# A transformer block on one core: five weight loads moved behind the first row reads, a modulation in ten pieces, scores head by head in two batches, and weight splits on GpSimd

## The chip, the cores and the metric

The kernel runs on one core of one Trainium2 chip. The metric is the time of one execution in device microseconds; lower is better. The core has five engines that run their own instruction lists and meet at semaphores: TensorE (PE; its weight loads are listed as PEld), VectorE (DVE), ScalarE (ACT), GpSimd (POOL) and SyncE (SP), which here only issues transfers.

## What is computed

One block of a conditioned transformer over 32 batches of 256 rows and 288 channels, in float32 precision (16 heads of 18 columns, inner width 1152):

```
ada = silu(c) @ W_ada + b_ada                 # c: one row of 288 for each batch
shift_msa, scale_msa, gate_msa, shift_mlp, scale_mlp, gate_mlp = split(ada, 6)
h = layernorm(x) * (1 + scale_msa) + shift_msa
q, k, v = split(h @ W_qkv + b_qkv)
attn = softmax(q * 18**-0.5 @ k.T)            # for each of 16 heads, 256 x 256
x = x + gate_msa * ((attn @ v) @ W_proj + b_proj)
h = layernorm(x) * (1 + scale_mlp) + shift_mlp
x = x + gate_mlp * (gelu(h @ W_fc1 + b_fc1) @ W_fc2 + b_fc2)
```

## The kernel before, in words

Float32 products are made of rounded parts: every operand is a rounded high part (`hi`) and the remainder (`lo`), and a product is high by high, high by low and low by high. So each weight is loaded in 12 transfers or groups of transfers (`loads`, numbered 0 to 11: 0 to 2 for W_qkv, 3 to 5 for W_proj, 6 to 8 for W_fc1, 9 to 11 for W_fc2), rounded on ACT (`round`) and split on DVE (`split`, L1035, or L1033 for the remainder rows 2, 5 and 8). All twelve loads are issued by SP before anything else of the batches; the loads 3 to 11 stand between the second batch's x and the first write of q and k.

A batch goes through steps that every engine knows by name. `ln1_stats` and `ln1_apply` normalise x; `xt` turns it on PE (L742, L745) and applies the modulation on ACT (L909); DVE and POOL make high and low parts (`xt` on these, POOL L1262). `qk` makes q and k (PE L768, 14 matmuls for a pair of tiles, ACT L918, DVE L1120), `v` makes v (L776). q and k are then written to memory as rows (`qkw`, SP L597, five writes) and read back in another layout (`qkr`, 24 reads, L613; six of those of the first half of batch 0 are issued by ACT, L990), `ql` and `kl` being the tiles that they land in. `s` is one pair of heads: four matmuls into two banks, head i of the pair in row half i of the array (L793). `max` is a head's maximum on DVE (L1128), `mt` turns the maxima and `mb` copies them into `ql` on ACT (L935), after which `st` (L810) makes the transposed scores, ACT the exponentials (L942) and `pv` (L822) the sums with v. `proj`, `lt`, `fc1`, `fc2` are the rest of the block.

`mod` is the second modulation (the columns of shift_mlp and scale_mlp for all batches) and `gate2`, `gate5` are the gates, all of them products of silu(c) with W_ada on PE (L715, L729). The first modulation is made by the same function before the batches begin. The first `st` waits for `gates_ready` and for both modulations.

The order in which each engine takes its steps is written out by hand in tables: a head for the first three periods (`PE_HEAD`, `ACT_HEAD`, `DVE_HEAD`, `POOL_HEAD`, `SYNC_HEAD`), a period that is repeated for the batches in the middle, and a tail. An engine never takes a step out of this order.

## Time and profile before

| | us |
|---|---|
| median of 3 runs | 1203.75 (1203.28 to 1208.13) |
| the profiled execution | 1203.89 |
| its span in the profile | 1202.1 |
| PE busy in the span | 1158.4 (96%) |
| DVE busy | 920.6 (77%) |
| ACT busy | 858.0 (71%) |
| POOL busy | 579.2 (48%) |
| mean granted TensorE clock | 0.984 of full speed |

The span is what the profile records of one execution. The time around it is 1.8 us. A share of busy time is a mean over stages which have different limits, so each stage is to be read by itself. The granted clock is a fraction of TensorE's upper level: 1.00 is the level of 2.4 GHz and 0.50 that of 1.2 GHz.

### The profile page before, as it was taken

Reading aid. Unit: us, or ns where it says so; the run is one execution under the profiler, and the core shown is the slowest. Engines: PE = TensorE matmul, PEld = TensorE weight load, DVE = VectorE, ACT = ScalarE, POOL = GpSimd, SP = SyncE. Lnnn points to the kernel's source line nnn. Section 1 sums busy time; section 2 is a strip of 40 time slices with the busy share of each in tenths; the row PEclk is TensorE's granted clock in tenths of the full one; section 3 lists DMA queues with packets and bytes.
Section 4 is the critical chain, followed back from the end, with each engine's and each line's share of the span. In section 5 each row is a group of like instructions: output and inputs, shape, how many; then the busy total and the mean of one; then the engine's idle time right before and its main releaser. Section 6 shows DMA issues by size and latency. Waiting matters only on the chain.

```text
span 1202.1 us, 28774 instructions
## 1 busy us (share of the span) xinstructions
PE 1158.4 (96%) x10375; PEld 993.9 (83%) x10375; DVE 920.6 (77%) x1928; ACT 858.0 (71%) x1485; POOL 579.2 (48%) x619
## 2 busy tenths in 40 slices
PE   6888999999999999999999999999999999999987
PEld 5666788888888888888888888888888888888777
DVE  5578878878878788887778888877888887877553
ACT  4378777777777777777777787777777777778721
POOL 3012444555544445554454555445455544544664
PEclk9779999999999999999999999999999999999999
DMA  9454554455555445555544555555445555444220
GB/s 276 137 172 156 163 164 147 150 175 168 164 159 163 149 148 173 166 171 164 163 151 151 159 179 165 165 159 167 143 149 181 164 165 161 158 148 156 83 68 20
DMA packets 133814, 186.93 MB, mean 156 GB/s; under 512 B 24284, under 2 KB 102150, under 8 KB 133675
## 3 DMA queue, kind: packets, MB, share of 16 engines
q1 hardware_dynamic: 133513, 184.66, 48.9%
q8 instruction: 84, 1.38, 0.5%
q10 hardware_dynamic: 162, 0.44, 0.1%
q14 instruction: 55, 0.45, 0.1%
HBM read 119.92 MB, written 64.60 MB: 153 GB/s over the span
## 4 chain that ended last, share of the span: by engine, by line
PE 92%; DVE 3%; ACT 2%; DMA 1%; issue 1%; SPq 0%; POOL 0%; ACTq 0%; POOLq 0%; DVEq 0%
PE a_bank L855 13%; PE x_bank L768 12%; PE turn_bank L822 10%; PE b_bank L855 9%; PE score_bank L793 7%; PE st_bank L810 7%; PE b_bank L869 7%; PE b_bank L870 6%; PE b_bank L871 6%; PE a_bank L836 5%; PE x_bank L776 5%; PE x_bank L742 2%; PE a_bank L742 1%; ACT e L942 1%; PE x_bank L745 1%
## 5 line engine op out<-in xcount | busy, mean ns | idle before, releaser
L1128 DVE TENSOR_REDUCE mx<-score_bank 128x2 f32<-128x512 f32 x512 | 332.3, 685 | 94.6 <-PE score_bank L793 92.8
L942 ACT ACTIVATE e<-st_bank 128x1024 f32<-128x1024 f32 x256 | 262.3, 1024 | 163.9 <-PE st_bank L810 163.3
L1285 POOL TENSOR_TENSOR gl<-gl_raw,gh 128x512 fp32r<-128x512 f32 (+1 forms) x160 | 197.2, 1241 | 180.8 <-DVE gh L1193 180.8
L935 ACT CAST ql<-mxt 4x256 fp32r<-4x256 f32 x512 | 205.7, 402 | 5.3
L869 PE MATMUL b_bank<-w,gh 128*128 128x288 f32 x576 | 179.1, 311 | 2.0 <-DVE tmp L1199 1.9
L870 PE MATMUL b_bank<-w,gh 128*128 128x288 f32 x576 | 170.6, 296 | 0.0
L871 PE MATMUL b_bank<-w,gl 128*128 128x288 f32 x576 | 169.6, 295 | 0.0
L822 PE MATMUL turn_bank<-e,ve 128*32 128x256 f32 x2048 | 125.8, 387 | 0.1
L810 PE MATMUL st_bank<-ql,kl 58*128 58x256 f32 x1024 | 117.9, 309 | 6.1 <-ACT e L942 5.0
L793 PE MATMUL score_bank<-kl,ql 58*128 58x256 f32 x1024 | 120.7, 314 | 2.7 <-DVE mx L1128 1.9
L855 PE MATMUL a_bank<-xh,w 128*128 128x256 f32 x640 | 112.2, 298 | 5.5 <-DVE xr L1107 4.0
L869 PEld LDWEIGHTS b_bank<-w,gh 128*128 128x128 f32 x576 | 108.6, 189 | 8.1 <-DVE tmp L1199 2.6
L1297 POOL TENSOR_TENSOR x<-tmp,x 128x288 f32<-128x288 f32 x64 | 52.0, 813 | 129.7 <-DVE tmp L1199 129.5
L768 PE MATMUL x_bank<-xh,wq 128*128 128x256 f32 x632 | 111.9, 300 | 2.2 <-DVE qst L1120 1.3
L1193 DVE CAST gh<-gl_raw 128x512 fp32r<-128x512 f32 (+1 forms) x160 | 92.7, 594 | 23.0 <-ACT gl_raw L980 22.0
L870 PEld LDWEIGHTS b_bank<-w,gh 128*128 128x128 f32 x576 | 108.7, 189 | 0.0
L871 PEld LDWEIGHTS b_bank<-w,gl 128*128 128x128 f32 x576 | 108.6, 189 | 0.0
L855 PEld LDWEIGHTS a_bank<-xh,w 128*128 128x128 f32 x640 | 87.4, 191 | 25.4 <-issue 15.1
L768 PEld LDWEIGHTS x_bank<-xh,wq 128*128 128x128 f32 x632 | 87.6, 193 | 20.2 <-issue 16.0
L793 PEld LDWEIGHTS score_bank<-kl,ql 58*128 58x128 f32 x1024 | 78.4, 188 | 30.9 <-issue 19.9
L810 PEld LDWEIGHTS st_bank<-ql,kl 58*128 58x128 f32 x1024 | 78.0, 187 | 29.8 <-issue 15.5
L822 PEld LDWEIGHTS turn_bank<-e,ve 128*32 128x32 f32 x2048 | 60.5, 111 | 43.9 <-issue 6.7
(152 smaller groups left out, 2490.9 us busy)
## 6 DMA issues: line engine op xcount, KB each, us to landing
qk_rows<-qst SPq DMA_DIRECT2D x128, 256.0 KB, 3.7
ql<-qk_rows SPq DMA_DIRECT2D x384, 72.0 KB
kl<-qk_rows SPq DMA_DIRECT2D x378, 72.0 KB
o_rows<-on SPq DMA_DIRECT2D x128, 128.0 KB
gate<-gates SPq DMA_DIRECT2D x32, 432.0 KB, 4.5
xin<-in_x SPq DMA_DIRECT2D x32, 288.0 KB, 4.1
x<-in_x SPq DMA_DIRECT2D x32, 288.0 KB, 4.0
out<-x SPq DMA_DIRECT2D x32, 288.0 KB, 2.2
```

The lines of the kernel that those rows point to most:

```text
L768: last = nc.tensor.matmul(bank[:, k * L:(k + 1) * L], wa[:, c * P:(c + 1) * P], xa, start=(i == 0), stop=(i == len(pr) - 1))
L793: last = nc.tensor.matmul(score_bank[i][:, t * L:(t + 1) * L], ql[rows, slot, j % HP, t * P:(t + 1) * P], kl[rows, slot, j % HP, :], start ...
L810: last = nc.tensor.matmul(st_bank[:, i, u, :], kl[rows, slot, j % HP, u * P:(u + 1) * P], ql[rows, slot, j % HP, :], start=True, stop=True)
L822: last = nc.tensor.matmul(turn_bank[VB * c:VB * (c + 1), q * L:(q + 1) * L], ve[:, b % 2, u, 8 * half + 2 * c + q, :], e[:, c, q, u, :], s ...
L855: last = nc.tensor.matmul(bank[:, (f % 2) * L:(f % 2 + 1) * L], wa[:, f * P:(f + 1) * P], xa, start=(i == 0), stop=(i == len(pr) - 1))
L869: nc.tensor.matmul(b_bank[:, 0:C], gh[:, cols], w2[:, 0, f, :], start=(f == 0), stop=False)
L870: nc.tensor.matmul(b_bank[:, 0:C], gh[:, cols], w2[:, 1, f, :], start=False, stop=False)
L871: last = nc.tensor.matmul(b_bank[:, 0:C], gl[:, cols], w2[:, 0, f, :], start=False, stop=(f == NF - 1))
L935: last = nc.scalar.copy(rows[:, :, :, a, :], src)
L942: nc.scalar.activation(e[:, j % 4, :, :, :].rearrange("p i u l -> p (i u l)"), st_bank[:, :, :, :].rearrange("p i u l -> p (i u l)"), ACT. ...
L1128: nc.vector.tensor_reduce(mx[:, j // HP, i, :, col:col + 1], score_bank[i][:, :].rearrange("p (t l) -> p t l", t=NT), AX.X, ALU.max).then_ ...
L1285: nc.gpsimd.tensor_tensor(gl[:, cols], g[:, cols], gh[:, cols].bitcast(F32), ALU.subtract).then_inc(g_lo, 1)
```

## The change

The tables of the head are rewritten, the periods and the tail are not. SP issues the loads 3 to 6 ahead of the batches and the loads 7 to 11 at places in its table. The second modulation is made in ten pieces, each of which is a step. The scores of the batches 0 and 1 are made by `sh`, one head at a time. Of the splits that stood in DVE's table only those of the remainder rows (5 and 8) stay there; the seven others are POOL's. In the function that makes a modulation, the three copies of the last 32 columns (`r`), which were the innermost loop, are now outside the loop over the rows of W_ada (`k`); the first modulation runs through it too.

```diff
-        N_FIRST = 3
+        N_FIRST, N_EARLY = 3, 7
...
-            for i in range(N_FIRST, len(loads)):
+            for i in range(N_FIRST, N_EARLY):
                 load_weights(i)
...
-            def mod_columns(n):
-                for i in range(2):
-                    c0 = MOD_OF[2 * n + i] * C
-                    for c in range(3):
-                        for k, (_r, nr) in enumerate(K_ROWS):
-                            rows = nr + (k == 2)
-                            for r in range(1 if c < 2 else 3):
-                                to = mod_of[n][:, i, c, :] if c < 2 else mod_of[n][REM * r:REM * (r + 1), i, c, :]
-                                cols = slice(c0 + c * P, min(c0 + (c + 1) * P, c0 + C))
-                                last = nc.tensor.matmul(to, w_ada_sb[k][0:rows, cols], sT[0:rows, k, :],
-                                                        start=(k == 0), stop=(k == 2))
-                last.then_inc(ada_mod, 1)
+            def mod_piece(n, i, c, r):
+                c0 = MOD_OF[2 * n + i] * C
+                cols = slice(c0 + c * P, min(c0 + (c + 1) * P, c0 + C))
+                for k, (_r, nr) in enumerate(K_ROWS):
+                    rows = nr + (k == 2)
+                    to = mod_of[n][:, i, c, :] if c < 2 else mod_of[n][REM * r:REM * (r + 1), i, c, :]
+                    last = nc.tensor.matmul(to, w_ada_sb[k][0:rows, cols], sT[0:rows, k, :],
+                                            start=(k == 0), stop=(k == 2))
+                return last
+            MOD_PIECES = [(i, c, r) for i in range(2) for c in range(3) for r in range(1 if c < 2 else 3)]
+            def mod_columns(n):
+                for i, c, r in MOD_PIECES:
+                    last = mod_piece(n, i, c, r)
+                last.then_inc(ada_mod, 1)
...
+            def s_head(b, h):
+                j, i = h // 2, h % 2
...
+                wait(pe, s_max[i], PAIRS * b + j)
+                rows = slice(TILE * i, TILE * i + KM)
+                for t in range(NT):
+                    last = nc.tensor.matmul(score_bank[i][:, t * L:(t + 1) * L],
+                                            ql[rows, slot, j % HP, t * P:(t + 1) * P], kl[rows, slot, j % HP, :],
+                                            start=True, stop=True)
+                last.then_inc(s_full[i], 1)
...
             def fc1(b, n):
                 if b == 0 and n == 0:
-                    act.wait_ge(w_split, len(loads))
+                    act.wait_ge(w_split, 5)
+                    act.wait_ge(w_late, 7)
...
+            def split_late(_b, i):
+                _kind, _w, _bias, raw, hi, lo, _n, _k = loads[i]
+                pool.wait_ge(w_hi, i + 1)
+                nc.gpsimd.tensor_tensor(lo, raw, hi.bitcast(F32), ALU.subtract).then_inc(w_late, 1)
```

The tables are shown by the instructions that they give, without those that come again. On PE, in the stretch that ends with the first scores, the kernel before has these rows (L715 is the second modulation, L745 the second part of `xt` of batch 1, L793 the first pair of scores):

```order
L715 MATMUL st_bank<-rcb,e 128x32 x2
L715 MATMUL st_bank<-rcb,gh_raw_56 128x32
L715 MATMUL st_bank<-rcb,e 128x32 x2
L715 MATMUL st_bank<-rcb,gh_raw_56 128x32
L715 MATMUL st_bank<-rcb,e 32x32 x6
L715 MATMUL st_bank<-rcb,gh_raw_56 32x32 x3
L745 MATMUL x_bank<-ident,xn 96x128 x2
L729 MATMUL a_bank<-e,rcb 32x288
L793 MATMUL score_bank0<-kl,ql 128x256
L793 MATMUL score_bank1<-kl,ql 128x256
L793 MATMUL score_bank0<-kl,ql 128x256
L793 MATMUL score_bank1<-kl,ql 128x256
```

The changed kernel has there (L718 is the modulation, L756 and L759 are `xt`, L743 the gates, L782 is `qk` of batch 1, L825 the new step for one head):

```order
L756 MATMUL x_bank<-ident,xn 128x128 x4
L718 MATMUL st_bank<-rcb,e 128x32 x2
L718 MATMUL st_bank<-rcb,gh_raw_56 128x32
L718 MATMUL st_bank<-rcb,e 32x32 x2
L718 MATMUL st_bank<-rcb,gh_raw_56 32x32
L759 MATMUL x_bank<-ident,xn 96x128 x2
L743 MATMUL a_bank<-e,rcb 32x288
L743 MATMUL b_bank<-e,rcb 32x288
L782 MATMUL x_bank<-xh1,wq 128x256 x4
```
```order
L782 MATMUL x_bank<-xl1,wq 128x256 x2
L782 MATMUL x_bank<-xr1,wq 128x256
L825 MATMUL score_bank0<-kl,ql 128x256 x2
L825 MATMUL score_bank1<-kl,ql 128x256 x2
L825 MATMUL score_bank0<-kl,ql 128x256 x2
```

Ahead of these one wide piece of the modulation now stands before `v` of batch 0. Two pieces are left between the two parts of `xt`, where ten were, and the other seven come after the first scores. The first scores stand behind the first 14 matmuls of `qk` of batch 1, where they stood ahead of them.

On SP, around the writes of q and k of batch 0, the kernel before has (L554 to L568 are loads of weights, L597 are the writes, L613 the reads, L573 are x of the batches 2 and 3):

```order
L554 DMA w1_raw_51<-in_L0_cond_W_fc1 128x1152 x2
L563 DMA gl_raw_57<-in_L0_cond_W_fc1 32x1152 x3
L565 DMA gl_raw_57<-in_L0_cond_b_fc1 1x1152 x2
L568 DMA w2_raw_52<-in_L0_cond_W_fc2 128x3x288 x3
L573 DMA xin<-in_x 128x576
L597 DMA qk_rows<-qst 128x2x256 x4
L597 DMA qk_rows<-qst 64x2x256
L613 DMA ql<-qk_rows 18x1024 x6
```

and the changed kernel (L560, L569 and L571 are the loads 7 and 8, L603 are writes, L619 reads, L579 is x):

```order
L603 DMA qk_rows<-qst 128x2x256 x2
L579 DMA xin<-in_x 128x576
L603 DMA qk_rows<-qst 128x2x256
L619 DMA ql<-qk_rows 18x1024
L579 DMA xin<-in_x 128x576
L603 DMA qk_rows<-qst 128x2x256
L619 DMA ql<-qk_rows 18x1024
L603 DMA qk_rows<-qst 64x2x256
L619 DMA ql<-qk_rows 18x1024 x4
L560 DMA w1_raw_51<-in_L0_cond_W_fc1 128x1152
L569 DMA gl_raw_57<-in_L0_cond_W_fc1 32x1152 x3
L571 DMA gl_raw_57<-in_L0_cond_b_fc1 1x1152 x2
```

Load 6 stands right ahead of these rows. So ten rows of weight transfers are gone from the place ahead of the writes. One of the loads of 128 by 1152 and the five small ones stand behind the first six reads, the loads of W_fc2 further on.

On POOL, at the layer norm and the turning of the batches 2 and 3, the kernel before has (L1236 are the inverse deviations that `ln1_apply` waits for, L1262 is `xt`, L1232 clears `ql`):

```order
L1262 TENSOR_TENSOR xl1<-xl1_raw_53,xh1 128x512
L1240 COPY mod1<-mod 128x6
L1236 TENSOR_TENSOR rs1<-ve1,mhalf 128x2
L1240 COPY mod1<-mod 128x6
L1236 TENSOR_TENSOR rs1<-ve1,mhalf 128x2
L1262 TENSOR_TENSOR xl1<-xl1_raw_53,xh1 128x512
L1232 MEMSET ql 68x1024 x2
L1262 TENSOR_TENSOR xl1<-xl1_raw_53,xh1 128x512
```

and the changed kernel (L1270 are the inverse deviations, L1301 is `xt`, L1297 the new split):

```order
L1297 TENSOR_TENSOR wp<-wp_raw_50,wp 126x288 x2
L1301 TENSOR_TENSOR xl1<-xl1_raw_53,xh1 128x512
L1274 COPY mod1<-mod 128x6
L1270 TENSOR_TENSOR rs1<-ve1,mhalf 128x2
L1301 TENSOR_TENSOR xl1<-xl1_raw_53,xh1 128x512
L1297 TENSOR_TENSOR w1<-w1_raw_51,w1 128x1152
L1274 COPY mod1<-mod 128x6
L1270 TENSOR_TENSOR rs1<-ve1,mhalf 128x2
L1297 TENSOR_TENSOR w1<-w1_raw_51,w1 128x1152
L1266 MEMSET ql 68x1024 x2
L1301 TENSOR_TENSOR xl1<-xl1_raw_53,xh1 128x512
```

So POOL has four splits of weights more in this stretch, two of them 1152 wide; the three splits of W_fc2 come later, the last one right behind the inverse deviations of batch 0's second layer norm.

## Rows read from the trace of the kernel before

**Rows 1.** Stretches of the span: length, each engine's busy time (instructions), granted clock, DMA share, GB/s.
```profile
20.00:30.00 10.00, 7.41 (x47) 6.26 (x45) 4.61 (x14) 2.25 (x5) 0.69 (x1) 1.00 1.05 283
30.00:45.00 15.00, 11.56 (x76) 9.32 (x77) 1.99 (x5) 2.41 (x5) 1.57 (x2) 0.56 0.56 151
45.00:58.00 13.00, 10.59 (x64) 7.43 (x62) 11.95 (x30) 6.58 (x13) 0.69 (x1) 0.89 0.38 118
58.00:73.00 15.00, 14.42 (x86) 9.35 (x86) 10.89 (x21) 10.28 (x19) 2.96 (x4) 0.51 0.57 177
93.00:140.00 47.00, 40.31 (x381) 30.69 (x380) 40.52 (x81) 38.97 (x71) 13.78 (x16) 0.96 0.48 151
140.00:1150.00 1010.00, 1007.43 (x9227) 872.36 (x9226) 801.76 (x1672) 762.41 (x1319) 521.37 (x547) 1.00 0.50 158
```

**Rows 2.** Chain that ended last, 6 to 24 us: start, length, what.
```profile
14.56 0.23 DVE xn L1056
...
14.84 1.13 PE x_bank L742 x4
...
17.22 0.65 PE x_bank L745 x2
...
18.66 3.24 PE x_bank L768 x14
```

**Rows 3.** The same chain over the whole span, two of its longest pieces.
```profile
25.17 6.93 DMA qk_rows<-qst
34.53 7.16 PE st_bank L715 x60
```

**Rows 4.** Instructions in time, 33 to 59 us: start, length, engine, line, what [idle before].
```profile
33.44 1.09 PE L742 MATMUL x_bank<-ident,xn 128*128 128x128 f32 x4 [4.67 <-ACT ve L924]
...
41.62 0.66 PE L745 MATMUL x_bank<-ident,xn 128*96 128x128 f32 x2
...
43.31 0.80 PE L793 MATMUL score_bank<-kl,ql 58*128 58x256 f32 x4
...
45.91 0.82 DVE L1041 BATCH_NORM_STATS2 stat<-xin 128x6 f32<-128x288 f32 x2
...
54.62 0.31 DVE L1137 STREAM_TRANSPOSE mxt<-mx 128x128 f32<-128x128 f32 x1
...
58.32 0.80 PE L810 MATMUL st_bank<-ql,kl 58*128 58x256 f32 x4
```

**Rows 5.** PE in time in the first modulation, two groups of narrow matmuls.
```profile
10.23 0.43 PE L715 MATMUL turn_bank<-rcb,e 128*32 128x32 f32 x12
10.60 0.33 PE L715 MATMUL turn_bank<-rcb,gh_raw 33*32 33x32 f32 x6
```

**Rows 6.** DVE by line and shape, 20 to 140 us: busy, mean ns, idle before.
```profile
L1128 DVE TENSOR_REDUCE mx<-score_bank 128x2 f32<-128x512 f32 x58 | 37.9, 684 | 11.7 <-PE score_bank L793 11.1
...
L1035 DVE TENSOR_TENSOR w<-w_raw,w 128x864 fp32r<-128x864 f32 x3 | 3.2, 1050 | 0.0
...
L1035 DVE TENSOR_TENSOR w<-w_raw,w 128x1152 fp32r<-128x1152 f32 x2 | 2.7, 1346 | 0.0
```

**Rows 7.** DVE and POOL in time, 67 to 70 us.
```profile
67.49 1.27 POOL L1262 TENSOR_TENSOR xl<-xl_raw,xh 128x512 fp32r<-128x512 f32 x1
67.63 2.18 DVE L1054 TENSOR_SCALAR xn<-xin,mv,rs 128x288 f32<-128x288 f32 x1 [0.21 <-POOL rs L1236]
...
68.70 0.94 POOL L1232 MEMSET ql<- 68x1024 f32 x1
```

**Rows 8.** A late row read on SP and the PE instruction that waited for it.
```profile
114.68 0.47 SPq L613 DMA_DIRECT2D kl<-qk_rows  x1
...
118.49 0.50 PE L793 MATMUL score_bank<-kl,ql 58*128 58x256 f32 x4 [0.65 <-DMA kl<-qk_rows]
```

**Rows 9.** DMA issues: size each, median us from issue to landing.
```profile
qk_rows<-qst SPq DMA_DIRECT2D x128, 256.0 KB, 3.7
```

**Rows 10.** L793 alone in 20 ns at the start of a pair of heads.
```profile
74.00:74.02 0.02, 0.01 (x2) 0.01 (x2) 1.00 0.00 0
```

125 lines of the change are left out of this document (70 added, 55 removed), and 56 rows, old and new, of tables (ACT_HEAD, DVE_HEAD, PE_HEAD, POOL_HEAD).

## The prediction

> **What bounds the kernel now.** I read the profile in this order: busy time by stretch, the chain that ended last, then instructions in time where the two show waits.
>
> In the stretch from 140 to 1150 us TensorE is busy 1007.4 of 1010 us at full clock [rows 1]. The tables of the periods and of the tail are the same in both kernels, so whatever TensorE reaches that stretch early or late by, the end moves by. The change can act only on the first 140 us. There the reader is to see three things. From 30 to 45 us the granted clock is 0.56, DVE works 2.0 and ACT 2.4 us of 15: all stand behind something. From 45 to 58 us DVE is busy 11.95 of 13 us and carries the stretch. From 58 to 73 us TensorE is busy 14.4 of 15 us, but at a granted clock of 0.51, the level of 1.2 GHz. From 93 to 140 us TensorE leaves 6.7 of 47 us idle and DVE 6.5 [rows 1].
>
> What all stand behind between 25 and 43 us is in the chain: the third write of q and k starts at 25.17 and takes 6.93 us, to 32.1; further on the second modulation takes 7.16 us in one piece [rows 3]. The DMA share between 20 and 30 us is 1.05, so the queues are full of weights [rows 1]. The median write of this kind lands in 3.7 us [rows 9]. In time: `xt` of batch 1 starts on TensorE at 33.44 after an idle time of 4.67 us, its second part at 41.62, the first scores at 43.31, DVE's first transposed maxima at 54.62, the first `st` at 58.32 [rows 4].
>
> **The change part by part.** Sums are made against the profiled execution, 1203.89 us, which is 0.1 us over the median shown.
>
> *The first modulation, a cost that the words of the change don't name.* The loop order changed: the three copies of the last 32 columns now follow one another, where they alternated. Alternating, 18 narrow matmuls of one half go in 0.7 us, 0.04 us each [rows 5]; the second modulation has 60 matmuls in 7.16 us, 36 of them narrow, so the 24 wide ones take (7.16 - 1.4) / 24 = 0.24 us each [rows 3, 5]. Narrow ones in a row that don't overlap cost between 0.04 (nothing changes) and 0.24 us (as a wide one). A narrow load has a quarter of the columns, so I take 0.06: 36 x 0.06 - 1.4 = 0.8 us. Nothing hides it: TensorE takes up `xt` at 14.84, right behind DVE's 14.56 + 0.23 [rows 2]. Term +0.8, bounds 0 and 7.
>
> The Trainium skill, "TensorEngine Tiling (Array Packing)", section Key Properties, says that different tiles of the array load weights and multiply in parallel. Rows 10 agree: two matmuls of a pair of heads and both their weight loads are in flight in the same 20 ns. By that rule alone both the narrow copies and the heads taken singly lose their overlap.
>
> *Five loads behind the reads.* By their shapes they take some 2.4 MB off the queues ahead of the writes. With an empty queue the third write takes the median 3.7 us instead of 6.93 [rows 3, 9]: with the 0.8 us above it lands at 25.17 + 0.8 + 3.7 = 29.7 instead of 32.1. The median is one of queues that are half busy (DMA share 0.50 in the steady stretch [rows 1]), so a little less is possible; the other bound is 6.93 (the queue isn't what held it).
>
> *The modulation in pieces.* `xt` of batch 1 started 1.3 us after the landing [rows 3, 4], so now at 31.0. Between its parts stood 8.2 us, 7.16 of them modulation [rows 3, 4]; one wide and one narrow piece are left, 1.0 us at this clock, and ACT has to take up the first part behind its 1.09 us on TensorE. So its second part comes at about 33.2. ACT still has to issue the last row read of the first half behind this, at about 34.5. A read issued at 114.68 freed its waiter at 118.49, 3.8 us later [rows 8]. So the reads have landed at 38.3. TensorE meanwhile does `qk` of batch 1: at the beginning 1.44 us lay between the second part of `xt` and `qk`, which took 3.24 us [rows 2]; 33.2 + 4.7 = 37.9, hidden behind the reads. First score 38.3 instead of 43.31: **-5.0 us**. Bounds: -7 (the reads have landed sooner and `qk` runs at the upper level in half of its 3.24 us) and 0.
>
> *From the first score to the first `st`*, 15.0 us [rows 4]. DVE carries it. The statistics of batch 2 (0.82 us and two small ones) and a split of 1.35 us [rows 4, 6] go out of it, some 2.5 us. Against it the gates on DVE now stand behind two wide and several narrow pieces on TensorE, which has 2.4 us idle in the stretch [rows 1]. **-2.0**, bounds -3 and +1.
>
> *Splits off DVE after that.* One of 1.35 and three of 1.05 us: 4.5 us [rows 6]. DVE is idle for 14% of 93 to 140 us [rows 1], and its in-order queue is only one of the three that TensorE waits for: I take 0.4 of it, **-1.7**, bounds -4.5 and 0.
>
> *The same splits on POOL.* 512 columns take 1.27 us there [rows 7], so 1152 take 2.9, 864 take 2.1 and 288 take 0.7: 13.5 us for seven. POOL is 48% busy and its queue is short here; the first GELU, which waits for all seven, is the last but one of ACT's steps in the head. But DVE is held: an operation from SBUF to SBUF, begun at 67.63, took 2.18 us and ended at 69.81, as POOL's two operations ended at 69.64 [rows 7]. The new splits of 2.9 and 2.1 us stand behind the inverse deviations that `ln1_apply` of batch 3 and `ln2_apply` of batch 0 wait for, so these meet them. Maxima read PSUM and aren't held: their mean over 58 groups is 685 ns with POOL busy or not [rows 6]. I take four meetings of 1 us, half of it on the path: **+2.0**, bounds 0 and 8.
>
> The Trainium skill, "SBUF — State Buffer", section "SBUF: two separate sides", says that the port pair that both engines share is an exclusive lock for a whole instruction, against a DVE operation in a two-port mode or with two SBUF inputs. By that rule the price of a meeting is up to the whole of POOL's 2.9 us; the trace agrees with the 2.18 us row.
>
> *Scores head by head.* A head waits for its own bank, not for both. DVE waited 11.1 us for scores between 20 and 140 us [rows 6]. Against it, TensorE pays for the lost overlap of a pair: two matmuls run at once before [rows 10]. **-1.5**, bounds -5 and +2.
>
> The steady stretch takes all of it over: -5.0 - 2.0 - 1.7 + 2.0 - 1.5 = -8.2 (the 0.8 is in the first term). 1203.9 - 8.2 = **1195.7**; I say 1195.5.
>
> **The rivals.**
>
> *More comes than the sum has: the clock stays up.* TensorE waits less between 25 and 45 us. If the stretch that ran at 0.51 with 14.4 us of work [rows 1] runs at the upper level, 7 us of work vanish, of which I count 4: 1191.5, down to 1185. Against it: in the stretch at 0.51 TensorE was 96% busy, so waits alone don't decide the level. Chance 0.17.
>
> *Given back on the way to 140 us.* POOL's lock at its full price: three meetings of 2.9, 2.9 and 2.1 us on the path, 7.9 instead of 2.0, gives 1195.5 + 5.9 = 1201.4. For it: the split of 2.9 us follows at once on the deviations. Or the stretch from 93 us on is set by ACT, whose work is unchanged (39.0 of 47 us busy, as much as DVE [rows 1]), and only the first term's half survives: about 1200. Chance 0.25.
>
> *The change doesn't do what it says:* the third write takes its 6.9 us also with the loads gone, because the first loads are still in the queues. Then the landing is at 32.9 and the first score 3 us later than I say: 1198.5. Held with the one above in the 0.25.
>
> *Slower: the clock falls for longer.* The work between 45 and 58 us ran at 0.89 (10.6 us busy) and that from 93 to 140 us at 0.96 (40.3 us busy) [rows 1]. Each us of it that runs at the lower level costs one more. To be slower than before by over 0.5% it has to cost 14 us above the sum, so more than 14 us of that work has to fall: with the first stretch at 0.5 and a tenth of the second, 1210 to 1214. For it: scores in single heads leave small gaps on TensorE. Against it: from 93 us on it was at 0.96 although TensorE idled 14% of the time. Chance 0.08.
>
> **How the numbers follow.** The sum's own case has 0.50 and runs from 1191.5 to 1199. Likeliest 1195.5. The range takes in the half of the better case and most of the given-back one: 1187 to 1201.5. A measurement of this kernel tells about 0.5% (6 us) from no change, so faster is below 1197.7: most of the main case (0.47) and the better one (0.17), 0.64; within 0.5% 0.28; slower 0.08.
>
> **What would show it.** Right: the third write lands near 30 us; `xt`'s second part at 33, first score near 38, first `st` near 51; the first modulation ends 0.8 us later; TensorE is saturated 8 us earlier and the steady period is unchanged. Wrong, if: `sh` waits for row reads behind the loads 7 and 8; DVE operations of over 2 us stand beside POOL's splits and a TensorE wait follows them; the granted clock shows more than some 30 us at 0.5 before 140 us; or the first modulation grew by several us.

## The result, and the profile after

The changed kernel takes 1220.76 us (median of 6 runs, 1215.02 to 1221.74) against 1203.93 us of the kernel before on the same chip: a ratio of 1.0123, 95% interval 1.0098 to 1.0148. It is 15 us slower. The forecast said 8 us faster, with a range of 1187 to 1201.5. The profiled execution took 1220.11 us, with a span of 1218.3.

The stretches of the kernel after, with the columns of [rows 1]:

```profile
20.00:30.00 10.00, 9.07 (x52) 8.33 (x52) 5.52 (x16) 2.83 (x6) 2.63 (x4) 1.00 0.35 110
30.00:45.00 15.00, 9.19 (x56) 6.57 (x56) 4.95 (x13) 4.27 (x8) 2.92 (x4) 0.91 0.77 187
45.00:58.00 13.00, 12.81 (x56) 9.68 (x55) 5.62 (x13) 5.12 (x11) 0.00 (x0) 0.50 0.71 215
58.00:73.00 15.00, 14.61 (x79) 11.08 (x82) 8.17 (x19) 6.53 (x10) 1.83 (x2) 0.50 0.56 165
73.00:93.00 20.00, 15.57 (x111) 11.15 (x115) 15.25 (x25) 11.27 (x20) 7.63 (x6) 0.67 0.39 117
93.00:110.00 17.00, 14.34 (x98) 10.15 (x94) 11.83 (x20) 10.90 (x20) 5.16 (x5) 0.70 0.42 129
110.00:140.00 30.00, 24.15 (x243) 17.03 (x236) 24.15 (x52) 25.55 (x47) 10.94 (x11) 0.99 0.48 144
140.00:1150.00 1010.00, 1007.09 (x9218) 871.49 (x9218) 809.62 (x1681) 766.71 (x1328) 515.56 (x542) 1.00 0.51 159
```

The steady stretch is what it was: TensorE busy 1007.1 of 1010 us at clock 1.00, 1007.4 before [rows 1]. All of the loss is ahead of it. The granted clock is lower there: from 45 to 73 us TensorE works at 0.50, the level of 1.2 GHz, and is 98% busy with it; before, the first 13 us of that ran at 0.89 [rows 1]. Between 73 and 110 us it is at 0.67 and 0.70. DVE, busy 11.95 us of the stretch from 45 to 58 us before, now has 5.62: the engine that carried this stretch now waits for TensorE.

What TensorE does with the time can be added up. The span is 16.2 us longer, so at 156.2 us this kernel has as much work left as the kernel before has at 140 (before, then after):

```profile
0.00:140.00 140.00, 110.91 (x863) 83.88 (x864) 97.69 (x214) 85.96 (x149) 31.38 (x47) 0.88 0.60 179
```
```profile
0.00:156.20 156.20, 127.27 (x877) 97.43 (x878) 99.06 (x208) 87.47 (x153) 41.70 (x51) 0.81 0.55 162
```

TensorE is idle for 29.1 us before and for 28.9 us after, so it does not wait longer; it is busy for longer. Of its busy time 32.0 us lay at the lower level before and 53.5 us lie there now. The first four matmuls of a `qk` tile take 1.22 us there and 0.64 at the upper level (at 44.03 and 45.62 in the kernel before), so I take half of the 21.5 us more as lost: an estimate of 10.8 of the 16.2 us. The other 5 to 6 us are work that takes longer at the same level, the copies of both modulations among it (below). This is an account of two single profiles. It says where the time is, and not yet which part of the change put it there.

The first modulation, and the first scores with what they waited for, PE in time:

```profile
10.24 0.42 PE L718 MATMUL turn_bank<-rcb,e 128*32 128x32 f32 x4
...
11.42 0.42 PE L718 MATMUL turn_bank<-rcb,e 128*32 128x32 f32 x4
11.77 0.31 PE L718 MATMUL turn_bank<-rcb,gh_raw 33*32 33x32 f32 x2
12.02 1.06 PE L718 MATMUL turn_bank<-rcb,e 128*128 128x32 f32 x4
...
16.90 1.11 PE L756 MATMUL x_bank<-ident,xn 128*128 128x128 f32 x4
...
32.09 0.63 PE L756 MATMUL x_bank<-ident,xn 128*128 128x128 f32 x4 [0.54 <-ACT ve L957]
...
34.01 0.40 PE L759 MATMUL x_bank<-ident,xn 128*96 128x128 f32 x2 [0.17 <-ACT xl_raw L942]
...
37.28 0.28 PE L782 MATMUL x_bank<-xr,wq 98*128 98x256 f32 x1
41.87 0.51 PE L825 MATMUL score_bank<-kl,ql 58*128 58x256 f32 x4 [4.31 <-DMA ql<-qk_rows]
...
62.18 0.58 PE L841 MATMUL st_bank<-ql,kl 58*128 58x256 f32 x1
```

SyncE's queue between the third write and the last reads:

```profile
27.70 0.36 SPq L603 DMA_DIRECT2D qk_rows<-qst  x1
...
30.90 0.35 SPq L579 DMA_DIRECT2D xin<-in_x  x1
31.30 0.43 SPq L603 DMA_DIRECT2D qk_rows<-qst  x1
...
32.20 0.71 SPq L603 DMA_DIRECT2D qk_rows<-qst  x1
32.96 2.06 SPq L619 DMA_DIRECT2D ql<-qk_rows  x4
35.06 0.37 SPq L560 DMA_DIRECT2D w_raw<-in_L_cond_W_fc  x1
...
36.86 0.57 SPq L571 DMA_DIRECT2D gl_raw<-in_L_cond_b_fc  x2
37.60 2.54 SPq L619 DMA_DIRECT2D ql<-qk_rows  x6
```

The first step came: the third write is issued at 27.70 and its first reader at 30.56, 2.5 us after the issue's end, where the landing took 6.93 us before [rows 3]; `xt` of batch 1 starts at 32.09 instead of 33.44, its second part at 34.01 instead of 41.62 [rows 4]. Then the head start is gone. `qk` is done at 37.6 and TensorE waits 4.31 us for row reads. Loads 7 and 8 are issued from 35.06 to 37.4, right behind the last read of the first half on SyncE and ahead of the second half's, so both share the DMA engines with them. The chain after holds the read that let TensorE go:

```profile
34.31 0.34 SPq L619
...
34.70 7.13 DMA ql<-qk_rows
```

That read took 7.13 us; the read of [rows 8] had freed its waiter after 3.8. First scores 41.87 instead of 43.31, first `st` 62.18 instead of 58.32 [rows 4].

The loads are not all that stands near this read. SyncE also issues x of batch 3 (30.90) and the last two writes (31.30 and 32.20) between the reads, and by the trace these land only at 34.94, 35.93 and 37.00. In the kernel before, both writes had landed by 33.15 and x went out behind the reads. So they are in flight together with the reads, as the loads are, and no run tests their places by themselves.

POOL's moved splits and what they did, all engines in time:

```profile
77.62 2.65 POOL L1297 TENSOR_TENSOR w<-w_raw,w 128x1152 fp32r<-128x1152 f32 x1
...
78.00 2.59 DVE L1067 SCALAR_TENSOR_TENSOR wp<-wp,minus_p,gl_raw 119x288 fp32r<-119x288 f32 x1
...
81.46 0.68 DVE L1154 TENSOR_TENSOR qst<-x_bank,qst 128x512 fp32r<-128x512 f32 x1
...
82.28 0.71 PE L782 MATMUL x_bank<-xh,wq 128*128 128x256 f32 x4 [3.21 <-DVE qst L1154]
```

DVE's remainder split of 119 rows by 288 columns takes 2.59 us and ends with POOL's (80.59 and 80.27). In the kernel before, the same instruction took 0.51 us with POOL idle:

```profile
49.78 0.51 DVE L1033 SCALAR_TENSOR_TENSOR wp<-wp,minus_p,gl_raw 119x288 fp32r<-119x288 f32 x1
```

Behind it stands the second half of a query-key tile, and TensorE waits 3.21 us for that. Not every such meeting costs: at 72.71 DVE's `xr` takes 2.74 us beside POOL's other wide split (72.40, 2.76 us), and TensorE, busy with `pv` until 76.56, waits for nothing behind it.

### The profile page after: what moved, and what is told of

It is laid out like the page before. It is cut to its first block, busy times and chain, and to the rows that moved or that the text cites. A ratio compares the mean times of both kernels' runs of the same rounds, so it can differ in the third digit from the quotient of the medians.

```text
span 1218.3 us, 28767 instructions
## 1 busy us (share of the span) xinstructions
PE 1174.5 (96%) x10375; PEld 1007.0 (83%) x10375; DVE 924.4 (76%) x1921; ACT 858.3 (70%) x1485; POOL 591.7 (49%) x626
## 4 chain that ended last, share of the span: by engine, by line
PE 91%; DVE 4%; ACT 2%; DMA 1%; issue 1%; SPq 1%; POOL 0%; POOLq 0%; DVEq 0%; ACTq 0%
PE a_bank L888 12%; PE x_bank L782 12%; PE turn_bank L853 9%; PE b_bank L888 9%; PE score_bank L807 7%; PE st_bank L841 7%; PE b_bank L902 7%; PE b_bank L903 6%; PE b_bank L904 6%; PE a_bank L868 5%; PE x_bank L790 5%; PE x_bank L756 1%; PE a_bank L756 1%; PE score_bank L825 1%; PE a_bank L759 1%
## 5 line engine op out<-in xcount | busy, mean ns | idle before, releaser
L841 PE MATMUL st_bank<-ql,kl 58*128 58x256 f32 x1024 | 121.3, 310 | 3.5 <-ACT e L975 2.5
L782 PE MATMUL x_bank<-xh,wq 128*128 128x256 f32 x632 | 114.2, 305 | 4.0 <-DVE qst L1154 3.2
L807 PE MATMUL score_bank<-kl,ql 58*128 58x256 f32 x960 | 111.9, 311 | 1.7 <-DMA kl<-qk_rows 1.0
L782 PEld LDWEIGHTS x_bank<-xh,wq 128*128 128x128 f32 x632 | 89.7, 197 | 21.9 <-issue 17.7
L841 PEld LDWEIGHTS st_bank<-ql,kl 58*128 58x128 f32 x1024 | 81.0, 189 | 25.3 <-issue 15.1
L807 PEld LDWEIGHTS score_bank<-kl,ql 58*128 58x128 f32 x960 | 72.5, 185 | 26.5 <-issue 16.4
```

The costliest lines, as they stand in the source:

```text
L782: last = nc.tensor.matmul(bank[:, k * L:(k + 1) * L], wa[:, c * P:(c + 1) * P], xa, start=(i == 0), stop=(i == len(pr) - 1))
L807: last = nc.tensor.matmul(score_bank[i][:, t * L:(t + 1) * L], ql[rows, slot, j % HP, t * P:(t + 1) * P], kl[rows, slot, j % HP, :], start ...
L841: last = nc.tensor.matmul(st_bank[:, i, u, :], kl[rows, slot, j % HP, u * P:(u + 1) * P], ql[rows, slot, j % HP, :], start=True, stop=True)
```

## The experiments

Each kernel is compared with the kernel before on the same chip. The medians of the kernel before lay between 1203.9 and 1206.2 us, so 0.001 is 1.2 us. Where a time inside one profile and the ratio disagree, the ratio counts: the profile is one execution. "Less" and "more" below compare a ratio with the 1.0123 of the changed kernel. Both have an interval of 0.002 to 0.003 to either side, so such a difference is uncertain by some 0.003, or 4 us; one of 3 to 4 us is not clear of noise. "Changed" and "before" name the kernel an edit starts from.

### One part of the change at a time

**loads_only.** Before, with loads 7 to 11 moved as in the change:

```diff
-            for i in range(N_FIRST, len(loads)):
+            for i in range(N_FIRST, N_EARLY):
...
-    ("qkr", 0, 5), ("ln1_stats", 3, 0), ("qkr", 0, 12)
+    ("qkr", 0, 5), ("ln1_stats", 3, 0), ("load", 0, 7), ("load", 0, 8), ("qkr", 0, 12)
```

> The kernel before with the loads 7 to 11 moved only: 7 and 8 behind the first six row reads of batch 0 and x of batch 3, 9 and 10 behind its last read, 11 in batch 2. If the queue full of weights held the third write of q and k, it lands near 28.9 us and not at 32.1, and since everything to the first scores follows it, the time is about 3 us under that of before (1200.5). Rival: the row reads now stand beside the loads 7 and 8 and land late (in the changed kernel the first scores waited 4.3 us for them); the second modulation on TensorE hides most of this here, and the time is within 1 us of before. Third: TensorE's idle time moves and the clock falls at another place, worth 3 us or more either way.

Ratio 0.9989 (0.9975 to 1.0002). The start of `xt` of batch 1 came at 30.86 instead of 33.44, the first `st` at 56.70 instead of 58.32. The loads alone are worth 1.3 us, not 5, and the interval holds no change.

**copies_in_a_row.** Before, with only the loop order of the first modulation (and of the second, which ran through the same function):

```diff
-                        for k, (_r, nr) in enumerate(K_ROWS):
-                            rows = nr + (k == 2)
-                            for r in range(1 if c < 2 else 3):
+                        for r in range(1 if c < 2 else 3):
+                            for k, (_r, nr) in enumerate(K_ROWS):
+                                rows = nr + (k == 2)
```

> The kernel before with only the loop order of the modulations changed (the three narrow copies one after another, in both modulations). The trace of the changed kernel shows the first modulation 2.1 us longer, with nothing to hide it. If this passes through, the time is 4 us over that of before (2.1 for the first modulation, 2 for the second, which stands on the path too). Rival: only the first counts, or the start's delay is taken up by the wait for the third write, whose queue is full of weights until about 31 us: then 0 to 2 us.

Ratio 1.0014 (0.9995 to 1.0033), so no cost is shown, and one of up to 4 us is not excluded. `xt` of batch 0 came 2.1 us later and `xt` of batch 1 not: before, TensorE waited 4.67 us there for the third write [rows 4], and that wait took the 2.1 us up. The second modulation grew too: the second part of `xt` of batch 1 came at 43.70 instead of 41.62.

**before_heads.** Before, with single heads for batches 0 and 1: each `("s", b, j)` becomes `("sh", b, 2j), ("sh", b, 2j+1)`.

> The kernel before with the scores of the batches 0 and 1 as single heads, one right behind the other, and nothing else. Pairs in the changed kernel made it 3.5 us slower, so single heads may be worth 2 to 3 us here as well: 1201.5. Rival: the gain there came from the places between the two heads, which don't exist here, and the overlap of the two row halves is lost: 0 to 2 us slower than before.

Ratio 0.9996 (0.9981 to 1.001). Nothing.

**before_splits_on_pool.** Before, with the seven late splits at places on POOL like the changed kernel's and nothing else:

```diff
-    ("ln1_stats", 1, 0), ("xt", 1, 0), ("ln1_stats", 2, 0), ("ln1_stats", 3, 0), ("xt", 2, 0), ("clr", 2, 0),
+    ("ln1_stats", 1, 0), ("split", 0, 3), ("split", 0, 4), ("xt", 1, 0), ("ln1_stats", 2, 0), ("ln1_stats", 3, 0), ("xt", 2, 0), ("split", 0, 6), ("clr", 2, 0), ("split", 0, 7),
...
+                nc.gpsimd.tensor_tensor(lo, raw, hi.bitcast(F32), ALU.subtract).then_inc(w_late, 1)
```

> The kernel before with the seven splits moved from DVE to GpSimd at places like those of the changed kernel, all else as before. If the hold on DVE is the dear part, it costs as in the changed kernel, 4 to 6 us: 1209 and DVE operations of over 2 us beside POOL's splits. Rival: here the statistics and the order are others, the holds fall on idle DVE time, and DVE's 5.4 us less make it 1 to 2 us faster.

Ratio 1.0089 (1.006 to 1.0118), 10.7 us. Alone in the kernel before, this part costs two thirds as much as the whole change. Its trace, POOL, DVE and PE in time:

```profile
69.56 2.69 POOL L1267 TENSOR_TENSOR w<-w_raw,w 128x1152 fp32r<-128x1152 f32 x1
69.68 3.51 DVE L1060 TENSOR_SCALAR xn<-xin,mv,rs 128x64 f32<-128x64 f32 x1
...
72.22 1.10 DVE L1108 CAST xr<-xl_raw 96x256 fp32r<-96x256 f32 x1
...
73.11 2.68 POOL L1267 TENSOR_TENSOR w<-w_raw,w 128x1152 fp32r<-128x1152 f32 x1
...
73.36 2.71 DVE L1111 TENSOR_TENSOR xr<-xl_raw,xr 32x256 fp32r<-32x256 f32 x1
...
76.12 0.58 PE L769 MATMUL x_bank<-xr,wq 98*128 98x256 f32 x1 [2.66 <-DVE xr L1111]
```

The small normalisation (128 x 64) has a mean of 0.31 us in the kernel before; here it holds DVE until the next instruction starts at 72.22, just as POOL's split ends. The remainder `xr` of 32 rows takes 2.71 us, and TensorE waits 2.66 us for it.

**before_pool_again.** Is it the hold, or do splits now come too late for those who need them? Before, its splits untouched on DVE, and besides seven POOL subtractions of the same shapes at the same places, into a buffer that nobody reads; POOL does 11 us more, and no one but POOL waits for it:

```diff
+                pool.wait_ge(w_hi, i + 1)
+                to = scratch[0:raw.shape[0], 0:raw.shape[-1]]
...
+                nc.gpsimd.tensor_tensor(to, hi.bitcast(F32), hi.bitcast(F32), ALU.subtract).then_inc(again_step, 1)
```

> The kernel before, its splits still on VectorE, and in addition seven GpSimd subtractions of the same shapes and at the same places in GpSimd's order as the moved splits, into a buffer that nobody reads. Nothing waits for them but GpSimd's own next instructions. Moving the seven splits to GpSimd in the kernel before had cost 10.7 us. Theory A (the hold: VectorE's and TensorE's delays come from what GpSimd's instructions do to VectorE's while they run): most of it is here too, +7 to +13 us, with VectorE instructions of 2 us or more that take 0.3 to 0.5 otherwise. Theory B (the splits come too late for the projections and the MLP that wait for them): 0 to +2 us, since nothing is late here. Theory C (GpSimd's own later work, as the second halves xl and the powers rs, is late behind them): +7 to +13 us too, but the waits of TensorE and VectorE that grow end in GpSimd's instructions and not in VectorE's long ones.

Ratio 1.0054 (1.0034 to 1.0075), 6.5 us. Nothing is late here but POOL, and yet more than half of the loss is there. Its trace at the same place:

```profile
68.70 2.17 POOL L1267 TENSOR_TENSOR scratch<-w 128x1152 f32<-128x1152 f32 x1
...
68.83 2.09 DVE L1058 TENSOR_SCALAR xn<-xin,mv,rs 128x64 f32<-128x64 f32 x1
...
71.78 2.14 POOL L1267 TENSOR_TENSOR scratch<-w 128x1152 f32<-128x1152 f32 x1
71.99 2.20 DVE L1109 TENSOR_TENSOR xr<-xl_raw,xr 32x256 fp32r<-32x256 f32 x1
...
74.25 0.39 PE L770 MATMUL x_bank<-xr,wq 98*128 98x256 f32 x1 [1.07 <-DVE xr L1109]
```

The same two DVE instructions are held, for 2.1 and 2.2 us behind POOL operations that here take 2.17 and 2.14 us, since both inputs are the same tensor. The hold grows with POOL's instruction. TensorE's wait behind it ends in DVE's `xr`, and from 20 to 140 us none of TensorE's waits ends in POOL, while DVE waits 0.5 us for it instead of 0.2. So TensorE pays for the hold, not for POOL's own lateness, and the third theory falls; the size lies just under what the first had said. The 4.2 us between 6.5 and 10.7 are at the edge of the noise, and no run parts the reasons that they can have: the longer instructions (11.7 us of five large ones against 9.6), late splits, or the clock. For the clock speaks that up to the same work left TensorE is idle for 32.9 us here and 33.3 us in before_splits_on_pool, but 37.7 us of its work lie at the lower level here and 49.0 us there.

### One part of the change taken back

**after_copies_alternate.** Changed, with the loop order of [rows 5] restored.

> The changed kernel with the three narrow copies alternating again; each modulation's copies of one half are made at the place of the last of the three pieces. First modulation 2.1 us shorter. If the delays add, 1217 (before 1203.9, changed 1220.8). Rival: the clock decides, and with the same idle time ahead of the first scores it falls in the same way: then no more than 2 us, or the fall comes at another time and moves the result by 5 us either way.

Ratio 1.0098 (1.0078 to 1.0117), 3.0 us less than the changed kernel, which is not clear of noise. The start of `xt` of batch 0 moved by only 0.3 us (it now waits 1.97 us for `xn`), and the first scores come later in this profile, at 43.21 instead of 41.87. So the first modulation's 2.1 us are not what is gained here, and I have no row that shows what is.

**after_loads_later.** Changed, with loads 7 and 8 behind the last row read of batch 0:

```diff
-    ("qkr", 0, 4), ("qkr", 0, 5), ("load", 0, 7), ("load", 0, 8), ("qkr", 0, 12),
+    ("qkr", 0, 4), ("qkr", 0, 5), ("qkr", 0, 12),
...
-    ("qkr", 0, 23), ("qkw", 1, 1), ("load", 0, 9), ("load", 0, 10),
+    ("qkr", 0, 23), ("qkw", 1, 1), ("load", 0, 7), ("load", 0, 8), ("load", 0, 9), ("load", 0, 10),
```

> The changed kernel with the loads 7 and 8 behind the last row read of batch 0, together with 9 and 10. If these loads held the row reads, the first scores start near 38.5 us instead of 41.87 and TensorE's wait of 4.3 us shrinks to 1. In the theory that this wait lets the clock fall for 34 us, the half-rate stretch from 42 us on is gone or short and the time falls to 1208 or less. Rival: the scores come earlier by 3 us and the time falls by that alone (1217.5), since the clock falls a little later all the same. Rival: the reads come no earlier, because what holds them is their own issue and landing: no change.

Ratio 1.0091 (1.007 to 1.0112), 3.9 us less, at the edge of the noise. The first scores, PE in time:

```profile
40.17 0.80 PE L825 MATMUL score_bank<-kl,ql 58*128 58x256 f32 x4 [2.37 <-DMA kl<-qk_rows]
```

They come at 40.17 instead of 41.87, and TensorE's wait is 2.37 instead of 4.31 us: the loads account for 1.7 us of the late reads. A wait of 2.37 us is left without them. And ScalarE now waits 5.27 us for load 7.

**after_splits_on_dve.** Changed, with the seven splits put back into DVE's order.

> The changed kernel with the seven splits of weights back on DVE, 3 and 4 early and the others behind steps of batches 1 to 3. In the changed kernel's trace two DVE operations of 0.5 us took 2.6 and 2.1 us beside a split on POOL, and TensorE then waited 3.2 and 1.9 us. If POOL's hold on DVE is dear, the time falls by 4 to 6 us, to about 1215.5, and no DVE operation of that kind is over 2 us before 110 us. Rival: DVE's own 4.5 us of splits cost as much, and the time stays within 2 us of 1220.8.

Ratio 1.0076 (1.0051 to 1.01), 5.7 us less, though DVE has its 5 us of work back.

**after_pairs.** Changed, with pairs of heads instead of single ones.

> The changed kernel with the scores of the batches 0 and 1 in pairs again, each pair at the place of its second head. If the lost overlap of the two row halves and the finer steps cost time, 1215 or less, above all through batch 1, where the changed kernel falls back by another 8 us. If single heads were a help against DVE's waits, the time grows to 1223 or more. If neither, it stays at 1219 to 1221.

Ratio 1.0152 (1.0123 to 1.0182), 3.5 us more, which is not clear of noise. If the single heads do anything in the changed kernel, they help. By its list of waits, PE waits 6.8 us for DVE's maxima between 30 and 93 us in this kernel.

**after_pieces_ahead.** Changed, with the last seven pieces of the second modulation and the third rows of gates in front of the first scores instead of between them:

```diff
-    ("sh", 0, 3), ("sh", 0, 4), ("mod", 0, 3), ("sh", 0, 5), ("mod", 0, 4), ("sh", 0, 6), ("sh", 0, 7), ("qk", 1, 2),
-    ("gate5", 0, 2), ("mod", 0, 5), ("mod", 0, 6), ("gate2", 0, 2), ("mod", 0, 7), ("mod", 0, 8), ("mod", 0, 9),
+    ("mod", 0, 3), ("mod", 0, 4), ("gate5", 0, 2), ("mod", 0, 5), ..., ("mod", 0, 9), ("sh", 0, 0), ...
```

> The changed kernel with the seven last pieces of the second modulation and the last rows of both gates ahead of the first scores, in the 4.3 us in which TensorE waited for the row reads. In the changed kernel they stand between the scores at the lower clock and take 7.5 us of TensorE from 48 to 60 us. If TensorE's queue is what makes the first st late, it comes at 56 to 58 us instead of 62.2 and the time falls by 4 to 6 us, to 1215. Rival: the gates' and maxima's order on DVE sets the first st, and the time falls by under 2 us.

Ratio 1.0069 (1.0047 to 1.0091), 6.5 us less. The first `st` starts at 58.68 instead of 62.18, 15.0 us behind the first scores (43.66), as before. In this kernel the scores wait for no DMA: the pieces fill the 4.3 us in which the reads are under way. In the changed kernel TensorE idles those 4.3 us and does the pieces afterwards, where it has no idle time and runs at the lower level:

```profile
53.11 1.17 PE L743 MATMUL b_bank<-gh_raw,rcb 33*32 33x288 f32 x2
54.21 1.06 PE L718 MATMUL st_bank<-rcb,e 128*128 128x32 f32 x4
...
55.76 1.06 PE L718 MATMUL st_bank<-rcb,e 128*128 128x32 f32 x4
...
57.32 1.16 PE L743 MATMUL a_bank<-gh_raw,rcb 33*32 33x288 f32 x2
58.41 0.42 PE L718 MATMUL st_bank<-rcb,e 128*32 128x32 f32 x4
...
60.19 1.33 PE L790 MATMUL x_bank<-wq,xh 128*128 128x288 f32 x4
```

From 53.11 to 60.19, 7.1 us of modulation and gates stand between the last query-key tile and `v` of batch 1, in front of the first `st`.

### Several parts

**after_three_undone.** Changed, with the copies, loads 7 and 8 and the splits taken back.

> The changed kernel with three things undone together: narrow copies alternate, the loads 7 and 8 behind batch 0's last read, the seven splits on DVE. Singly they gave 1.23% down to 0.98%, 0.91% and 0.76% above before. If they are separate costs, together they give 1.23 - 0.25 - 0.32 - 0.47 = 0.19% above before, 1206 where before is 1204. Rival: they are the same few us counted thrice (all of them the clock's luck): then 0.7% above, 1212.

Ratio 1.0037 (1.0018 to 1.0057). The three together give back 10.4 us; singly 3.0, 3.9 and 5.7, a sum of 12.6. That is no difference within the noise, so they may well be separate costs.

**after_copies_splits.** The same with the loads left where the change puts them.

> The changed kernel with two parts taken back: narrow copies alternate again and the seven late splits stand on VectorE; loads 7 and 8 stay ahead of the first batch's last reads. With these two and the loads undone it was 1.0037, with the pieces as well 1.0046; in both ScalarE waited 4.9 to 5.9 us for load 8. Theory A (late loads gain at the first scores what they lose at ScalarE's rounding): 1.002 to 1.005, the first scores 2 us or more later than with three undone, but no such wait of ScalarE. Theory B (each part's share adds: 1.0123 less 0.0025 less 0.0047): 1.005 to 1.007.

Ratio 1.0064 (1.0042 to 1.0086), as the second theory has it. The two give back 7 us, singly 8.7; moving the two loads is worth 3 us beside them (1.0037 against 1.0064), again at the edge of the noise. First scores come at 42.24, after a wait of 3.66 us for `kl`.

**after_four_undone.** The three, and the pieces ahead as well.

> The changed kernel with four parts taken back: narrow copies alternate again, loads 7 and 8 behind the first batch's last read, the seven late splits on VectorE, and the last seven pieces of the second modulation with both third rows of gates ahead of the first scores. What is left of the change is loads 3 to 6 ahead and the rest behind the reads, the first three pieces and the single heads. Theory A (the four parts make up the loss): taken back singly they gave back 3.0, 2.7, 5.6 and 6.4 us, three together 11.0 of a sum of 11.3; with the fourth it is about as fast as the kernel before, 0.997 to 1.001, with the first st before 58 us. Theory B (the pieces and the late splits are two views of one delay, so that they don't add): no faster than with three undone, 1.002 to 1.005. Theory C (the loss sits in what is left, the single heads or the load order): 1.005 or more.

Ratio 1.0046 (1.0026 to 1.0065): no better than with three, against my first theory. The pieces were worth 6.5 us alone and nothing here, and this difference is clear of the noise. The number is the second theory's, which named pieces and splits as the pair that doesn't add. I take it to be another, pieces and loads: the pieces fill a wait that is longest while loads 7 and 8 stand right behind the reads. No run has the pieces and the loads alone moved back, so this is argued from the rows. With the loads moved back, the scores come at 40.76 without a wait, and the waits that are left are behind load 7: ScalarE waits 5.9 us for it, and TensorE 2.65 us for the query-key tile that is rounded behind it.

### The clock

**after_filled.** Is TensorE's idle time at 37 to 42 us what brings the clock down? Changed, with forty matmuls of 128 x 256 in that wait, into a bank that is free then; nobody reads them:

```diff
-    ("qk", 1, 0), ("sh", 0, 0),
+    ("qk", 1, 0), ("fill", 0, 40), ("sh", 0, 0),
```

> The changed kernel with 40 extra matmuls of 128 by 256 (wq by wq, their result is used by nobody) on TensorE between qk of batch 1 and the first scores, where it waited 4.3 us. Theory that the clock is the cause: the granted clock doesn't fall at 42 us, the stretch from 45 to 73 us runs at 1.00, the first st comes at 57 to 59 us instead of 62.2 and the time is 1211 or less. Rival, that the new order itself is slow (scores, pieces and gates stand in each other's way whatever the clock): the clock stays up for the stretch and the time is within 3 us of the changed kernel (1218 to 1222). Second rival: the clock falls all the same a few us later, nothing changes.

Ratio 1.0104 (1.0082 to 1.0126), intervals overlap with the changed kernel's. The stretches of this kernel:

```profile
30.00:45.00 15.00, 13.35 (x98) 10.89 (x97) 4.82 (x12) 4.28 (x8) 2.91 (x4) 1.00 0.76 181
45.00:58.00 13.00, 12.20 (x67) 8.59 (x65) 6.88 (x16) 5.12 (x11) 0.00 (x0) 0.66 0.73 227
58.00:73.00 15.00, 14.61 (x80) 10.87 (x82) 8.71 (x17) 8.03 (x14) 3.38 (x2) 0.50 0.54 162
73.00:93.00 20.00, 16.27 (x103) 12.25 (x99) 14.40 (x27) 10.45 (x18) 6.08 (x6) 0.59 0.39 117
```

TensorE is busy 13.35 of 15 us at clock 1.00 up to 45 us, and then it falls all the same, 7 us later than in the changed kernel, and from 58 to 73 us it is busy 14.61 us at 0.50. Filling the wait only postpones the fall in this profile.

**before_filled.** The same forty matmuls in front of `xt` of batch 1 in the kernel before.

> The kernel before with 40 extra matmuls of 128 by 256 (result used by nobody) ahead of xt of batch 1, where TensorE waited 4.7 us. If the clock is what such a wait costs, the second modulation runs at the upper level, takes 3.7 us instead of 7.2, and the first st comes 4 us earlier: about 1200 against 1204 of before, or more if the clock also stays up later. Rival: the clock falls a few us later for as long as before, and the time is the same within 1.5 us.

Ratio 0.9981 (0.9966 to 0.9996). Its profile has 24 us at the lower level up to 140 us, where the profile before has 34.

### Do the harmless parts make a faster kernel?

**before_best.** Before, with the forty matmuls, single heads, and loads 7 to 11 moved, 7 and 8 behind the first batch's last read.

> The kernel before with the pieces that were no loss: loads 7 to 11 moved into SP's order, but 7 and 8 behind the first batch's last read, the heads of two batches scored singly, and forty matmuls of full rows ahead of the second batch's first transpose, whose results nobody reads. Theory A (they add): loads alone gave 1.3 us and the forty matmuls 2.3, single heads 0.5; together 0.996 to 0.998 of the kernel before. Theory B (each of them only shortens the same wait for the third write and the reads): 0.998 to 0.999, no better than the best of them. Theory C (the single heads behind a TensorE at full rate are held by their own waits for VectorE): 1.000 or more.

Ratio 1.005 (1.0033 to 1.0066), 6 us slower. Only the third theory allows for that, and its mechanism, the single heads, is not the one. ACT and PE in time show it:

```profile
54.88 1.15 ACT L911 CAST w<-w_raw 128x1152 fp32r<-128x1152 f32 x1 [9.26 <-DMA w_raw<-in_L_cond_W_fc]
...
57.39 1.19 PE L768 MATMUL x_bank<-xh,wq 128*128 128x256 f32 x4 [8.09 <-DVE qst L1142]
```

ScalarE's order in the kernel before rounds load 7 ahead of the second query-key tile of batch 1. (It is load 7 that is waited for; the expectations of these kernels call it load 8, which follows it at once.) The load is issued at 48.94, ScalarE waits 9.26 us for it, and DVE and TensorE (8.09 us) wait behind. In the changed kernel that rounding stands one query-key tile later; I had moved the transfer without its reader. The last kernel below differs from this one only in the place of loads 7 and 8, and has 0.9994: the late loads cost 0.0056, 7 us.

**before_loads_filled.** The same with loads 7 and 8 at the changed kernel's place, and pairs of heads.

> The kernel before with loads 7 to 11 at the changed kernel's places (7 and 8 ahead of the first batch's last reads) and forty matmuls ahead of the second batch's first transpose, whose results nobody reads. In before_best load 8 came so late that ScalarE waited 9.3 us for it, with the rounding of the second batch's first query-key tile queued behind; here it is early again. Theory A (the gains of loads_only, 1.3 us, and of before_filled, 2.3 us, add; before_best lost its time in that wait): 0.996 to 0.998, and no wait of ScalarE for load 8. Theory B (both only shorten the wait in front of the second transposes, so the forty matmuls now lie in its place): 0.998 to 1.000.

Ratio 1.0 (0.9984 to 1.0016), the second theory's. ScalarE no longer waits for the load. The gain of before_filled (0.0019) is not there again, as it would be if the two shorten one and the same wait; the intervals overlap, so this isn't shown.

**before_loads_filled_heads.** The same with single heads.

> The same with single heads for the first two batches. Theory A (before_best's loss was all the late load): within 0.1% of before_loads_filled, 0.996 to 0.998. Theory B (the single heads lose time where the clock is up, since each waits for VectorE's maximum of the same bank): 1.000 to 1.004.

Ratio 0.9994 (0.9981 to 1.0008): single heads cost nothing here either. No version that ran is faster than the kernel before by more than its interval, but for before_filled by 0.2%, which the two last kernels don't bear out.

## Why the prediction was wrong

Of the things that would show it wrong, the prediction's last part had all four: `sh` waits behind loads 7 and 8, DVE instructions of over 2 us beside POOL's splits, 55 us at the lower level before 140 us, and a first modulation 2.1 us longer (it had said several us). Each was given too small a price or too small a chance. By its steps:

- **First modulation, +0.8.** It cost 2.06 us: `xt` of batch 0 at 16.90 instead of 14.84 [rows 2]. A narrow copy in a row takes 0.10 us (18 in 1.78 us), not 0.06. The argument from the fewer columns was wrong: what counted was that the copies alternate (0.04 us each [rows 5]) or don't. What it costs at the end is not shown: 1.7 us in the kernel before, where a wait stood behind it (copies_in_a_row), and 3.0 us in the changed one, neither clear of noise. The narrow matmuls of the second modulation had no term at all, and the second part of `xt` came 2.1 us later in copies_in_a_row.
- **Third write lands at 29.7.** Its first reader is issued at 30.56. The landing was quicker than I took it (2.5 us against 3.7), the write 2.9 us later than before, 2.1 of them by the copies. Moving the loads did what it says.
- **First scores at 38.3, -5.0.** 41.87, -1.4. This is where the sum failed first. The step "a read issued freed its waiter 3.8 us later" was taken from a stretch in which no loads were in flight. Here the read took 7.13 us, with loads 7 and 8 issued right behind it; with them away the scores came at 40.17 (after_loads_later), so they make 1.7 of the 3.6 us that were missing. I had named this as a sign of failure and given it no term. The other 1.9 us stay open; x of batch 3 and two writes, which the new order puts between the reads, are an untested reason.
- **First score to first `st`, -2.0.** It became +5.3 (20.3 us instead of 15.0). "DVE carries it" was a row of before, and the change undid what it rested on: TensorE's pieces and gates, some 7.7 us at the lower level (0.59 at 49.60 and 7.1 from 53.11), went into a stretch where I counted 2.4 us of TensorE idle time. After_pieces_ahead brings the 15.0 us back, and 6.5 us of the end. This is the mechanism that I had only as a remark about gates.
- **Splits off DVE -1.7 and on POOL +2.0.** The sum had +0.3 us for the two. Together they cost 5.7 us in the changed kernel and 10.7 us alone in the kernel before. The hold was right, its size not: I had counted meetings of 1 us, half on the path. A meeting lasts as long as POOL's instruction, 2.1 to 2.7 us, there are several, and what is held are steps that TensorE waits for at once (`xr`, the second half of `qk`). The upper bound of the term, 8, was nearer than its value. "Given back by POOL's lock" was the rival whose mechanism came, but I put it at 1201.4 since I let it act on a sum that was itself 8 us too good.
- **Single heads, -1.5.** Not contradicted: -3.5 in the changed kernel, inside its bounds but not clear of noise, and nothing in the kernel before.
- **The clock.** The rival "slower: the clock falls for longer" had 0.08. Its condition came: 55 us at the lower level ahead of 140 us instead of 34. By the account above it is the largest part of the loss: 53.5 us of TensorE's work at the lower level instead of 32.0, some 10.8 us. The reason that I had given for it, small gaps between single heads, is not borne out: before_heads makes single heads too and has 27 us at the lower level. Its price is not a term beside the others, though: with the loads, the pieces or the splits taken back 49, 51 and 44 us lie at the lower level up to 140 us instead of 55 (with the copies 55 as well), so what those parts cost includes some of it.

The Trainium skill, "SBUF — State Buffer", section "SBUF: two separate sides", says that whichever of the two starts first has the port pair for the whole instruction and the other blocks. By that the price of a meeting is up to POOL's whole instruction, and the trace agrees (2.65 us of POOL, 2.59 us of a DVE operation that takes 0.51). The prediction named this price and used it only in a bound and a rival; its term went by an average of 1 us, for which it gave no row.

Does the account close? The four parts taken back singly give 3.0 + 3.9 + 5.7 + 6.5 = 19.1 us, more than the 15 us lost, with an uncertainty that alone would allow for that. Clear of it are the splits and the pieces, and that the pieces give nothing once the other three are back. Taken together the four give back 9.3 and leave 5.5 us (1.0046). Of that, after_four_undone shows one part, load 7 too late for ScalarE, which cost 7 us in before_best. Not run was the changed kernel with copies, splits and pieces taken back and the loads left early, which would decide it, nor one with the old places of x and the writes on SyncE. What makes the granted clock fall stays open as well: the fill shows only that TensorE's idle time just ahead of the fall isn't needed for it. Single profiles of kernels whose ratio is 1.000 (before_heads and before) differ by 7 us of time at the lower level, so I draw no more from it.

## What to carry to other kernels

Work of the bounding engine that lies in a wait is free, and costs its full time, at the clock granted there, once it is cut up and spread over a stretch in which that engine is busy: before dividing such a block, look at which wait covers it. Moving work from VectorE to GpSimd saves VectorE's time only if no SBUF-to-SBUF operation of VectorE's meets it; count each meeting at GpSimd's full duration and ask which engine waits for what stands behind. Bulk loads right behind small reads that an engine waits for are not out of their way (here 1.7 us at the first scores), and when a load is moved, the place in its reader's order has to move with it.

## What the hardware showed that I had not expected

- VectorE's operations from SBUF to SBUF are held also when they have a single tensor input: the normalisation of 128 x 64, 0.31 us otherwise, ran 3.51 us in its record beside a split of 2.69 us and the clearing behind it. The maxima, which read PSUM, kept their mean of 0.68 us.
- Two subtractions of equal shape on GpSimd differ by their inputs: 2.68 us for 128 x 1152 with two tensors, 2.15 us where both inputs are one tensor and the output is not rounded.
- Narrow matmuls (32 columns, 32 wide) that alternate between three column groups take 0.04 us each [rows 5], one group after the other 0.10 us.
- TensorE stays at the lower level while it is 97 to 99% busy: 12.81 of 13 and 14.61 of 15 us in the kernel after.
